# A state-space layer in a four-layer kernel: residual rows through TensorE, the norm's sums on ScalarE, two projections one slot sooner, one product moved from GpSimd to VectorE

## The chip, the cores and the metric

One core of a Trainium2 chip runs one program. The metric is the device time of a run in microseconds (us), the median over several runs. The core's engines are TensorE (PE in the profile; PEld is its weight load), VectorE (DVE), ScalarE (ACT), GpSimd (POOL) and SyncE (SP, which issues the DMAs). Engines work through their own instruction lists and meet only at semaphores.

## The reference, cut to what matters

The whole network is attention, a mixture of experts, a state-space layer and another mixture of experts on 8 sequences of 512 tokens by 256 features. The change is in the third, the state-space layer:

```python
h  = layernorm(layernorm(x)) * ln_g + ln_b           # over 256 features
xi, z = split(h @ W_in.T)                            # 512 channels each
u  = silu(conv4(xi) + conv_b)
dt, B, C = split(u @ W_x.T);  dt = softplus(dt @ W_dt + b_dt)
hst[t] = exp(dt[t] * A) * hst[t-1] + (dt[t] * u[t]) * B[t]     # 16 states for each channel
y[t] = sum over the 16 states of hst[t] * C[t]
out = x + (layernorm(x) + ((y + u * Dp) * silu(z)) @ W_out.T)
```

## The kernel before, in words

`mamba_phase` holds the layer. A **batch** m is one sequence (512 tokens; 8 batches). Its 512 channels are 4 channel tiles of 128 partitions, and the 16 states of a tile are 8 pairs, so a batch is 32 **units** of one tile and one pair of states; there are 256 units. The recurrence of a unit is one scan of VectorE over 2 x 512 elements.

A unit q passes these engines: ScalarE makes the decays `mb_da_ps` (L1817 to L1819: one zero, two Exp, two PSUM buffers taken in turn); GpSimd makes the added terms `mb_dbu` (L1769); VectorE scans; the scanned states are multiplied with C; TensorE sums the products into `mb_y_ps` (L1953: identity times product, two matmuls of 512 columns, each two records in the trace). The multiplication is done by VectorE (L1902 scan in place, L1908 product into `mb_hc`, two buffers) for pairs 0, 2, 4, 6 and 7, and by GpSimd (L1900 scan into `mb_hp`, three buffers, L1775 product) for pairs 1, 3 and 5.

Everything else of the layer is a list of small tasks, hung into the 32 **slots** of a batch by the table `SCHEDULE`: `(kind, index, ahead)`, where `ahead` says for which batch the task is (0: this one; 1: the next; 2: the one after it; -1: the last one). Every engine walks the same slots in order. TensorE does the tasks of a slot s after the sums of slot s (unit s-1 where VectorE multiplied, unit s-3 where GpSimd did); ScalarE does them after the decays of unit s+3, VectorE after unit s+3 (it is written `tasks(s - 3)` on VectorE, `tasks(s - 2)` on ScalarE). `EARLY_SCHEDULES` changes the table for the lead-in (n = -1) and the first batch (n = 0).

The kinds that matter here:

- `ln`: mean and variance of a batch's rows; `rsqrt`, `newton`, `norm_r`, `norm_h` follow. `norm_r` writes `mb_res`, the row that is to be added at the end; `norm_h` writes the normed input over `mb_xin`.
- `tr` 0 and 1: TensorE transposes `mb_xin` (L1965, 4 blocks each), ScalarE and VectorE split the result into `mb_hT_hi` and `mb_hT_lo`.
- `xi` 0 to 3, `z` 0 to 3: input projections (L1972, 6 matmuls each); `conv_a`, `conv`: half a convolution each (L1976); `xd`, `dt`: the small projections.
- `dt` i: TensorE, then five ScalarE instructions, then three of VectorE (the last is L1936).
- `out_a`, `out`: output projection of the last batch, 4 matmuls of 256 columns each (L1989); after each pair VectorE adds the result to `mb_res` (L1940), and SP stores when both are added.
- `final` i: VectorE multiplies a tile's sum `mb_y_ps` with silu(z) (L1914). It needs all 8 units of the tile summed by TensorE. Final i belongs to slot 6, 14, 22 or 30, so VectorE does final 0, 1, 2 after units 9, 17, 25 and final 3 after unit 1 of the next batch.

All task matmuls write into two PSUM buffers `mb_f_ps` taken in turn, in the order of the table: a fill may start when the fill two before it has been read out (`f_used`). So the order of the table decides which engine's reading a fill waits for.

Of the kernel before, what the change touches and what calls it, by code (L numbers as in the profile page):

```python
# [1635 lines left out]
LATER = (("z", 0, 1), ("z", 1, 1), ("z", 2, 1), ("z", 3, 1), ("norm_h", 0, 2), ("silu_z", 0, 1))
MOVED = {24: LATER[4:5], 25: LATER[0:2], 26: LATER[2:4]}
EARLY_SCHEDULES = {-1: {at: [task for task in SCHEDULE[at] if task not in LATER] + list(MOVED.get(at, ())) for at in SCHEDULE},
                   0: {at: SCHEDULE[at] + [("silu_z", 0, 0)] * (at == 1) for at in SCHEDULE}}
# [3 lines left out]
def mamba_phase(nc, sem, A, layer, x_in, x_out):  # L1643

    with ExitStack() as ctx:
# [78 lines left out]
        with nc.Block() as block:  # L1724
# [159 lines left out]
            def _(dve):  # L1884
# [5 lines left out]
                for s in SLOTS:  # L1890
# [18 lines left out]
                    for kind, i, m in tasks(s - 3):  # L1909
# [5 lines left out]
                        if kind == "ln":  # L1915
                            dve.wait_ge(S["x_loaded"], 16 * (m + 1))
                            wait(dve, S["h_ready"], m)
                            for k in range(4):
                                dve.bn_stats(stats[:, k, :], xin[:, k, :]).then_inc(S["stats_done"], 1)
                            dve.wait_ge(S["stats_done"], 4 * m + 4)  # L1920
                            for k in range(4):
                                last = dve.bn_aggr(mv[:, k, :], stats[:, k, :])
# [160 lines left out]
```

## Time and profile before

| | us |
|---|---|
| median of 3 runs | 2292.87 |
| lowest, highest | 2292.38, 2293.6 |
| the profiled execution: its own time | 2300.35 |
| the profiled execution: span of the trace | 2298.6 |

The profiled execution is 7.5 us (0.33%) above the median of the runs. Busy shares of its span: TensorE 84%, VectorE 74%, GpSimd 62%, ScalarE 52%. The state-space layer lies from 1015.6 to about 1998 us. Its loop over the units starts with the first scan at 1081.7 us and ends with the last final at 1988.8 us. Before it stands the lead-in (norms, projections and convolution of batch 0, transposes of batch 1), after it the last output projection.

Timeline rows give start, duration, engine, line, operation, tiles, shapes, how many instructions are merged, and in brackets the idle time of the engine before the row with what ended it. The distance between the starts of two rows on one engine is what the first one costs that engine's list.

### The profile page before, as it was taken

What the parts mean: (1) busy time and instruction counts of PE and PEld (TensorE: products, weight loads), DVE (VectorE), ACT (ScalarE), POOL (GpSimd) and SP (SyncE); (2) the same over time, 40 slices, a digit from 0 to 9 for tenths busy, and PEclk for the clock granted to TensorE, in tenths of its full rate; (3) what the DMA queues carried; (4) which work ended last, traced back from release to release, by engine and by line L of the source; (5) the groups of instructions that cost most, each with busy time, mean ns of one, the idle gap of its engine ahead of it and who ended that gap; (6) DMA issues with size and microseconds to landing.
All of it is one profiled execution on the core that took longest, in us unless ns stands there. A gap on an engine that the chain in (4) does not pass through costs nothing. (4 is left out here: it accounts for less than half of the span.)

```text
span 2298.6 us, 32626 instructions
## 1 busy us (share of the span) xinstructions
PE 1941.0 (84%) x9846; PEld 1136.6 (49%) x9846; DVE 1694.2 (74%) x2406; ACT 1198.6 (52%) x2466; POOL 1430.1 (62%) x1164
## 2 busy tenths in 40 slices
PE   2499999999873999947989898989898987569998
PEld 1234444444433999933444444444444433257776
DVE  4488777787744656522999999999999999655654
ACT  1066666666652433325676767676767574223222
POOL 7334435543342444422999999999999999444444
PEclk9699989898876999978999999999999999879999
DMA  3554444453143544424040404040404040101110
GB/s 81 103 110 101 103 96 108 111 124 100 51 153 127 100 70 75 76 39 157 0 148 19 148 19 148 19 148 19 148 19 148 10 148 9 60 7 37 36 36 19
DMA packets 231216, 185.57 MB, mean 81 GB/s; under 512 B 148729, under 2 KB 201601, under 8 KB 231058
## 3 DMA queue, kind: packets, MB, share of 16 engines
q1 hardware_dynamic: 216178, 162.61, 25.1%
q0 software_dynamic: 13296, 17.77, 4.4%
q10 hardware_dynamic: 1584, 3.24, 0.4%
q8 instruction: 80, 1.31, 0.2%
q14 instruction: 78, 0.64, 0.1%
HBM read 134.07 MB, written 49.49 MB: 80 GB/s over the span
## 5 line engine op out<-in xcount | busy, mean ns | idle before, releaser
L1769 POOL TENSOR_TENSOR mb_dbu<-mb_dtu,mb_bbc 128x1024 f32<-128x1024 f32 x256 | 600.4, 2361 | 41.8 <-DVE mb_hp L1900 29.6
L473 ACT ACTIVATE ex_plain<-at_t_ps 128x512 f32<-128x512 f32 x512 | 289.4, 595 | 185.9 <-PE at_t_ps L851 180.7
L1902 DVE TENSOR_TENSOR_SCAN mb_da_ps<-mb_da_ps,mb_dbu 128x1024 f32<-128x1024 f32 x160 | 365.3, 2283 | 12.6 <-ACT mb_da_ps L1819 12.6
L1953 PE MATMUL mb_y_ps<-mb_hc,lw_ident 128*128 128x512 f32 x640 | 323.9, 631 | 57.2 <-DVE mb_hc L1908 57.2
L610 DVE TENSOR_REDUCE at_mx<-at_s_ps 128x2 f32<-128x1024 f32 x256 | 310.8, 1219 | 51.4 <-PE at_s_ps L860 49.1
L860 PE MATMUL at_s_ps<-ex_w 48*128 48x512 f32 x512 | 228.1, 507 | 38.4 <-DVE at_mx L610 24.9
L851 PE MATMUL at_t_ps<-ex_w 64*128 64x512 f32 x512 | 221.7, 490 | 12.6 <-ACT ex_plain L473 6.7
L1953 PEld LDWEIGHTS mb_y_ps<-mb_hc,lw_ident 128*128 128x128 f32 x640 | 123.7, 199 | 215.7 <-issue 127.0
L1775 POOL TENSOR_TENSOR mb_hp<-mb_hp,mb_cbc 128x1024 f32<-128x1024 f32 x96 | 226.6, 2361 | 0.0
...
L1900 DVE TENSOR_TENSOR_SCAN mb_hp<-mb_da_ps,mb_dbu 128x1024 f32<-128x1024 f32 x96 | 218.8, 2279 | 2.5 <-ACT mb_da_ps L1819 2.5
L1908 DVE TENSOR_TENSOR mb_hc<-mb_da_ps,mb_cbc 128x1024 f32<-128x1024 f32 x160 | 196.0, 1225 | 18.3 <-DVE mb_da_ps L1902 0.5
L1817 ACT ACTIVATE mb_da_ps<-mb_zero 128x1 f32<-128x1 f32 x256 | 43.3, 169 | 289.0 <-DVE mb_hc L1908 240.2
L1953 PE MATMUL mb_y_ps<-mb_hp,lw_ident 128*128 128x512 f32 x384 | 190.9, 621 | 0.0
L851 PEld LDWEIGHTS at_t_ps<-ex_w 64*128 64x128 f32 x512 | 87.6, 195 | 172.7 <-ACT ex_plain L473 127.9
L1818 ACT ACTIVATE mb_da_ps<-mb_dt,lw_a_neg 128x512 f32<-128x512 f32 x256 | 172.5, 674 | 0.1
L1819 ACT ACTIVATE mb_da_ps<-mb_dt,lw_a_neg 128x511 f32<-128x511 f32 x256 | 171.8, 671 | 0.0
L1300 PE MATMUL m_y_ps<-ex_w,m_xsT_hi 128*128 x568 | 156.8, 337 | 0.0
L1415 POOL TENSOR_TENSOR m_odd<-m_odd,m_odd_in 128x256 f32<-128x256 f32 x96 | 70.8, 738 | 133.3 <-ACT m_odd_in L1473 130.0
L871 PE MATMUL at_o_ps<-ex_plain 128*32 128x512 f32 x1024 | 146.7, 646 | 0.1
L422 POOL CAST at_qk_hi<-at_qk 128x512 fp32r<-128x512 f32 x32 | 19.6, 611 | 185.8 <-DVE at_qk L754 185.8
L860 PEld LDWEIGHTS at_s_ps<-ex_w 48*128 48x128 f32 x512 | 89.6, 198 | 58.7 <-DVE at_mx L610 37.3
...
## 6 DMA issues: line engine op xcount, KB each, us to landing
...
```

The costliest lines, as they stand in the source:

```text
L473: act.activation(probs[:, c, h, :], t_ps[:, k % 2, :], ACT.Exp, scale=SCALE).then_inc(exp_done, 1)
L610: dve.tensor_reduce(out, s_ps[:, m % 2, :, :], AX.X, ALU.max).then_inc(max_done, 1)
L851: pe.matmul(t_ps[:, k % 2, :], of_head(kst, r, h, 64, c), of_head(qst, r, h, 64), start=True, stop=True).then_inc(t_ready, 1)
L860: last = pe.matmul(s_ps[:, m % 2, a, :], of_head(qst, u % 4, h + 2 * a, 48, c), of_head(kst, u % 4, h + 2 * a, 48), start=True, stop=True)
L1769: pool.tensor_tensor(dbu[:, q % 3, :, :], dtu_2, bbc[:, 2 * p:2 * p + 2, :], ALU.mult).then_inc(S["dbu_ready"], 1)
L1775: pool.tensor_tensor(hp[:, r, :, :], hp[:, r, :, :], cbc[:, 2 * p:2 * p + 2, :], ALU.mult).then_inc(S["hp_ready"], 1)
L1818: act.activation(da_ps[:, q % 2, 0, :], dt[:, d % 2, :], ACT.Exp, scale=a_neg[:, d, 2 * p:2 * p + 1])
L1819: act.activation(da_ps[:, q % 2, 1, 1:T], dt[:, d % 2, 1:T], ACT.Exp, scale=a_neg[:, d, 2 * p + 1:2 * p + 2]).then_inc(S["da_ready"], 1)
L1900: dve.tensor_tensor_scan(hp[:, t % 3, :, :].rearrange("p j t -> p (j t)"), da, add, 0.0, ALU.mult, ALU.add).then_inc(S["scan_done"], 1)
L1902: dve.tensor_tensor_scan(da, da, add, 0.0, ALU.mult, ALU.add).then_inc(S["scan_done"], 1)
L1908: dve.tensor_tensor(hc[:, t % 2, :, :], da_ps[:, r, :, :], cbc[:, 2 * p:2 * p + 2, :], ALU.mult).then_inc(S["hc_ready"], 1)
L1953: last = pe.matmul(y_ps[:, v % 2, :], ident[:, :], src[:, j, :], start=False, stop=(q == tile_last[v] and j == 1))
```

## The change

Four edits, all in `mamba_phase` and its table:

1. **The residual row.** TensorE starts each group of output matmuls with one more matmul, identity times the rows of `mb_res` (256 columns), so the PSUM result holds the sum already. VectorE's addition (L1940) goes; ScalarE copies the result into `mb_res` instead, in its own slot order.
2. **The norm's sums.** VectorE's `bn_stats` and `bn_aggr` (L1919, L1922) go. ScalarE takes sums as a by-product of three instructions for each of the four row blocks: a Copy with scale 1/256 whose sum is the mean, a small one for minus the mean over 16, and a Square whose sum is the variance. They hang in slots 10 to 13, one block each, where before one `ln` task hung in slot 11.
3. **The table.** `xi` 0 and 1 of the batch after next go from slots 31 and 0 to 30 and 31; the transposes `tr` from slot 27 to 26; `z` 3 from slot 26 to 24, so ahead of `dt` 0 of slot 25.
4. **Who multiplies.** Unit 19 of each batch (tile 2, pair 3) goes from GpSimd to VectorE, which leaves GpSimd 11 of 32.

```diff
-POOL_PAIRS = (1, 3, 5)
+POOL_UNITS = tuple(q for q in range(NU) if q % NP in (1, 3, 5) and q != 19)
...
-    25: [("dt", 0, 1), ("bb", 2, 1), ("cb", 0, 1)], 26: [("z", 3, 1), ("bb", 3, 1), ("cb", 1, 1)], 27: [("tr", 0, 2), ("tr", 1, 2), ("bb", 4, 1), ("cb", 2, 1)],
+    25: [("dt", 0, 1), ("bb", 2, 1), ("cb", 0, 1)], 26: [("tr", 0, 2), ("tr", 1, 2), ("bb", 3, 1), ("cb", 1, 1)], 27: [("bb", 4, 1), ("cb", 2, 1)],
...
-    31: [("xi", 0, 2), ("cb", 6, 1), ("cb", 7, 1)],
+    31: [("xi", 1, 2), ("cb", 6, 1), ("cb", 7, 1)],
...
+MOVED = {24: [("norm_h", 0, 2)], 25: [("z", 0, 1), ("z", 1, 1)], 26: [("z", 2, 1), ("z", 3, 1)], 27: [("tr", 0, 2), ("tr", 1, 2)], 31: [("xi", 0, 2)]}
+LATER = [task for at in MOVED for task in MOVED[at]] + [("xi", 1, 2), ("silu_z", 0, 1)]
+EARLY_SCHEDULES = {-1: {at: [task for task in SCHEDULE[at] if task not in LATER] + MOVED.get(at, []) for at in SCHEDULE},
+                   0: {at: [("xi", 1, 1)] * (at == 1) + SCHEDULE[at] + [("silu_z", 0, 0)] * (at == 1) for at in SCHEDULE}}
...
         def by_pool(q):
-            return q % NP in POOL_PAIRS
+            return q % NU in POOL_UNITS
...
@@ ScalarE
+                        if kind == "ln":
+                            act.wait_ge(S["x_loaded"], 16 * (m + 1))
+                            wait(act, S["x_stored"], 16 * (m - 2))
+                            act.activation(res[:, m % 3, i, :], xin[:, i, :], ACT.Copy, scale=1.0 / D, accum_out=mv[:, i, 0:1]).then_inc(S["stats_done"], 1)
+                            act.wait_ge(S["stats_done"], 12 * m + 3 * i + 1)
+                            act.activation(nm[:, i:i + 1], mv[:, i, 0:1], ACT.Copy, scale=-1.0 / 16.0).then_inc(S["stats_done"], 1)
+                            act.wait_ge(S["stats_done"], 12 * m + 3 * i + 2)
+                            act.activation(res[:, m % 3, i, :], xin[:, i, :], ACT.Square, scale=1.0 / 16.0, bias=nm[:, i:i + 1], accum_out=mv[:, i, 1:2]).then_inc(S["stats_done"], 1)
                         if kind == "rsqrt":
-                            act.wait_ge(S["var_ready"], m + 1)
+                            act.wait_ge(S["stats_done"], 12 * m + 12)
...
+                        if kind == "out":
+                            f, used = filled(act, "out", i, m)
+                            act.activation(res[:, m % 3, 2 * i:2 * i + 2, :], f.rearrange("p (a c) -> p a c", a=2), ACT.Copy).then_inc(used, 1)
@@ VectorE
-                        if kind == "ln":
...
-                        if kind == "out":
-                            f, used = filled(dve, "out", i, m)
-                            r_2 = res[:, m % 3, 2 * i:2 * i + 2, :]
-                            dve.tensor_tensor(r_2, f.rearrange("p (a c) -> p a c", a=2), r_2, ALU.add).then_inc(used, 1)
@@ TensorE
                         if whole == "out":
+                            pe.matmul(out[:, a * D:(a + 1) * D], ident[:, :], res[:, m % 3, 2 * i + a, :], start=True, stop=False)
                             for d in range(ND):
-                                last = pe.matmul(out[:, a * D:(a + 1) * D], u[:, m % 2, d, tok], wo[:, d, :], start=(d == 0), stop=(d == ND - 1))
+                                last = pe.matmul(out[:, a * D:(a + 1) * D], u[:, m % 2, d, tok], wo[:, d, :], start=False, stop=(d == ND - 1))
```

TensorE's list around the transposes, in a batch of the loop, before. `mb_hc` rows are sums of VectorE's products, `mb_hp` rows of GpSimd's, the row from `mb_xin` is the eight transposes:

```order
L1972 MATMUL mb_f_ps<-mb_hT_lo,lw_wi_hi 128x512
L1953 MATMUL mb_y_ps<-mb_hc,lw_ident 128x512 x2
L1965 MATMUL mb_f_ps<-lw_ident,mb_xin 128x128 x8
L1953 MATMUL mb_y_ps<-mb_hp,lw_ident 128x512 x2
L1953 MATMUL mb_y_ps<-mb_hc,lw_ident 128x512 x2
```

The same place after the change, with the last row ahead of the transposes being `dt` 0:

```order
L1948 MATMUL mb_y_ps<-mb_u,lw_diag_d 128x512
L1951 MATMUL mb_y_ps<-mb_hc,lw_ident 128x512 x2
L1981 MATMUL mb_f_ps<-mb_xd,lw_wdt 128x512
L1963 MATMUL mb_f_ps<-lw_ident,mb_xin 128x128 x8
L1951 MATMUL mb_y_ps<-mb_hc,lw_ident 128x512 x2
L1951 MATMUL mb_y_ps<-mb_hp,lw_ident 128x512 x2
```

The sum of unit 26 stood ahead of the transposes and now stands behind them; `z` 3 has gone ahead of `dt` 0.

TensorE's list at the turn to the next batch, before: the sums of units 31 and 29, which complete tile 3, then the six matmuls of `xi` 1, then the next tile's first matmul:

```order
L1953 MATMUL mb_y_ps<-mb_hc,lw_ident 128x512 x2
L1953 MATMUL mb_y_ps<-mb_hp,lw_ident 128x512 x2
L1972 MATMUL mb_f_ps<-mb_hT_hi,lw_wi_hi 128x512
L1972 MATMUL mb_f_ps<-mb_hT_hi,lw_wi_lo 128x512
L1972 MATMUL mb_f_ps<-mb_hT_lo,lw_wi_hi 128x512
L1972 MATMUL mb_f_ps<-mb_hT_hi,lw_wi_hi 128x512
L1972 MATMUL mb_f_ps<-mb_hT_hi,lw_wi_lo 128x512
L1972 MATMUL mb_f_ps<-mb_hT_lo,lw_wi_hi 128x512
L1950 MATMUL mb_y_ps<-mb_u,lw_diag_d 128x512
```

The same place after, from the sum of unit 30 on:

```order
L1951 MATMUL mb_y_ps<-mb_hc,lw_ident 128x512 x2
L1970 MATMUL mb_f_ps<-mb_hT_hi,lw_wi_hi 128x512
L1970 MATMUL mb_f_ps<-mb_hT_hi,lw_wi_lo 128x512
L1970 MATMUL mb_f_ps<-mb_hT_lo,lw_wi_hi 128x512
L1970 MATMUL mb_f_ps<-mb_hT_hi,lw_wi_hi 128x512
L1970 MATMUL mb_f_ps<-mb_hT_hi,lw_wi_lo 128x512
L1970 MATMUL mb_f_ps<-mb_hT_lo,lw_wi_hi 128x512
L1951 MATMUL mb_y_ps<-mb_hc,lw_ident 128x512 x2
L1951 MATMUL mb_y_ps<-mb_hp,lw_ident 128x512 x2
L1948 MATMUL mb_y_ps<-mb_u,lw_diag_d 128x512
```

`xi` 1 stood behind the sums of units 31 and 29 and now stands ahead of them.

TensorE's list at the end of the output projection of a batch, before:

```order
L1989 MATMUL mb_f_ps<-lw_wo,mb_u 128x256 x4
L1953 MATMUL mb_y_ps<-mb_hc,lw_ident 128x512 x2
L1989 MATMUL mb_f_ps<-lw_wo,mb_u 128x256 x4
L1953 MATMUL mb_y_ps<-mb_hp,lw_ident 128x512 x2
L1976 MATMUL mb_f_ps<-mb_xi,lw_diag 128x512 x2
```

and after:

```order
L1986 MATMUL mb_f_ps<-mb_res,lw_ident 128x256
L1988 MATMUL mb_f_ps<-lw_wo,mb_u 128x256 x4
L1951 MATMUL mb_y_ps<-mb_hc,lw_ident 128x512 x2
L1986 MATMUL mb_f_ps<-mb_res,lw_ident 128x256
L1988 MATMUL mb_f_ps<-lw_wo,mb_u 128x256 x4
L1951 MATMUL mb_y_ps<-mb_hp,lw_ident 128x512 x2
L1974 MATMUL mb_f_ps<-mb_xi,lw_diag 128x512 x2
```

One matmul of 256 columns has come in ahead of each group of four; nothing else has moved there.

## Rows read from the trace of the kernel before

**Rows 1.** Busy time by stretch: PE, PEld, DVE, ACT, POOL; clock, DMA share, GB/s

```profile
1230.00:1258.00 28.00, 28.00 (x73) 13.23 (x72) 27.38 (x25) 17.46 (x38) 27.28 (x15) 1.00 0.08 23
1298.00:1316.00 18.00, 16.39 (x43) 9.02 (x44) 17.59 (x14) 13.31 (x24) 16.20 (x9) 0.81 0.67 238
```

**Rows 2.** Waits from 1100 to 1990 us: total us, times, longest

```profile
ACT mb_da_ps L1817 <- DVE mb_hc L1908: 236.3, 112, 4.2
```

**Rows 3.** Timeline of VectorE, units 13 to 15 of a batch

```profile
1585.05 2.28 DVE L1900 TENSOR_TENSOR_SCAN mb_hp<-mb_da_ps,mb_dbu 128x1024 f32<-128x1024 f32 x1
1587.25 2.27 DVE L1902 TENSOR_TENSOR_SCAN mb_da_ps<-mb_da_ps,mb_dbu 128x1024 f32<-128x1024 f32 x1
1589.62 1.23 DVE L1908 TENSOR_TENSOR mb_hc<-mb_da_ps,mb_cbc 128x1024 f32<-128x1024 f32 x1
1590.76 1.40 DVE L1919 BATCH_NORM_STATS2 mb_stats<-mb_xin 128x6 f32<-128x256 f32 x4
...
1592.49 2.26 DVE L1902 TENSOR_TENSOR_SCAN mb_da_ps<-mb_da_ps,mb_dbu 128x1024 f32<-128x1024 f32 x1
```

**Rows 4.** Timeline from dt 1 to final 0 of the same batch

```profile
1556.32 0.69 DVE L1936 TENSOR_TENSOR mb_dt<-mb_f_ps,mb_dt 128x512 f32<-128x512 f32 x1
...
1557.06 1.99 PE L1989 MATMUL mb_f_ps<-lw_wo,mb_u 128*128 128x256 f32 x8 [0.81 <-DVE mb_dt L1936]
...
1562.67 0.68 DVE L1940 TENSOR_TENSOR mb_res<-mb_f_ps,mb_res 128x512 f32<-128x512 f32 x1
...
1570.92 1.88 PE L1953 MATMUL mb_y_ps<-mb_hp,lw_ident 128*128 128x512 f32 x4
...
1573.16 0.66 DVE L1914 TENSOR_TENSOR mb_u<-mb_y_ps,mb_z 128x512 f32<-128x512 f32 x1
```

**Rows 5.** Timeline at final 1: tile 1's last sum, and the final

```profile
1597.97 1.88 PE L1953 MATMUL mb_y_ps<-mb_hp,lw_ident 128*128 128x512 f32 x4
...
1601.73 0.67 DVE L1914 TENSOR_TENSOR mb_u<-mb_y_ps,mb_z 128x512 f32<-128x512 f32 x1
```

**Rows 6.** Timeline from dt 0 to final 3: transposes, tile 3's last sum

```profile
1641.66 0.69 DVE L1936 TENSOR_TENSOR mb_dt<-mb_f_ps,mb_dt 128x512 f32<-128x512 f32 x1
...
1642.40 1.97 PE L1965 MATMUL mb_f_ps<-lw_ident,mb_xin 128*128 128x128 f32 x8 [5.37 <-DVE mb_dt L1936]
...
1650.51 1.88 PE L1953 MATMUL mb_y_ps<-mb_hc,lw_ident 128*128 128x512 f32 x4
...
1653.61 1.88 PE L1953 MATMUL mb_y_ps<-mb_hc,lw_ident 128*128 128x512 f32 x4
...
1655.33 1.88 PE L1953 MATMUL mb_y_ps<-mb_hp,lw_ident 128*128 128x512 f32 x4
...
1658.47 0.67 DVE L1914 TENSOR_TENSOR mb_u<-mb_y_ps,mb_z 128x512 f32<-128x512 f32 x1
```

**Rows 7.** The same two anchors in an earlier batch

```profile
1298.87 0.69 DVE L1936 TENSOR_TENSOR mb_dt<-mb_f_ps,mb_dt 128x512 f32<-128x512 f32 x1
...
1313.27 1.88 PE L1953 MATMUL mb_y_ps<-mb_hp,lw_ident 128*128 128x512 f32 x4
```

**Rows 8.** Timeline at the end of the layer's loop

```profile
1986.87 1.88 PE L1953 MATMUL mb_y_ps<-mb_hp,lw_ident 128*128 128x512 f32 x4
1988.79 0.69 DVE L1914 TENSOR_TENSOR mb_u<-mb_y_ps,mb_z 128x512 f32<-128x512 f32 x1 [3.79 <-PE mb_y_ps L1953]
1989.63 7.14 PE L1989 MATMUL mb_f_ps<-lw_wo,mb_u 128*128 128x256 f32 x32 [0.87 <-DVE mb_u L1914]
```

**Rows 9.** Timeline of ScalarE: a norm_r task, four row blocks

```profile
1607.35 2.06 ACT L1833 ACTIVATE mb_res<-mb_xin,mb_nb,mb_up 128x256 f32<-128x256 f32 x4
```

**Rows 10.** Timeline of the lead-in: batch 0's sums, first reader, first late scan

```profile
1019.51 1.41 DVE L1919 BATCH_NORM_STATS2 mb_stats<-mb_xin 128x6 f32<-128x256 f32 x4 [2.07 <-DMA mb_xin<-x]
...
1021.45 0.30 ACT L1823 ACTIVATE mb_av<-mb_mv,mb_fix 128x4 f32<-128x4 f32 x1 [4.23 <-DVE mb_mv L1922]
...
1101.32 2.29 DVE L1900 TENSOR_TENSOR_SCAN mb_hp<-mb_da_ps,mb_dbu 128x1024 f32<-128x1024 f32 x1 [2.47 <-ACT mb_da_ps L1819]
```

More of the change, by code:

```diff
@@ L1622 @@
 NU = ND * NP
-POOL_PAIRS = (1, 3, 5)
+POOL_UNITS = tuple(q for q in range(NU) if q % NP in (1, 3, 5) and q != 19)
 SCHEDULE = {
-    0: [("xi", 1, 1)], 1: [("dt", 1, 0)], 2: [("out_a", 0, -1)], 3: [("out", 0, -1)], 4: [("out_a", 1, -1)], 5: [("out", 1, -1)],
-    6: [("conv_a", 0, 1), ("final", 0, 0)], 7: [("conv", 0, 1)], 8: [("dt", 2, 0), ("load", 0, 2)], 9: [("conv_a", 1, 1)], 10: [("conv", 1, 1)],
-    11: [("xi", 2, 1), ("ln", 0, 2)], 12: [("xi", 3, 1)], 13: [("z", 0, 1), ("newton", 0, 2)], 14: [("conv_a", 2, 1), ("final", 1, 0), ("rsqrt", 0, 2)],
+    1: [("dt", 1, 0)], 2: [("out_a", 0, -1)], 3: [("out", 0, -1)], 4: [("out_a", 1, -1)], 5: [("out", 1, -1)],
+    6: [("conv_a", 0, 1), ("final", 0, 0)], 7: [("conv", 0, 1)], 8: [("dt", 2, 0), ("load", 0, 2)], 9: [("conv_a", 1, 1)], 10: [("conv", 1, 1), ("ln", 0, 2)],
+    11: [("xi", 2, 1), ("ln", 1, 2)], 12: [("xi", 3, 1), ("ln", 2, 2)], 13: [("z", 0, 1), ("ln", 3, 2), ("newton", 0, 2)], 14: [("conv_a", 2, 1), ("final", 1, 0), ("rsqrt", 0, 2)],
     15: [("conv", 2, 1)], 16: [("dt", 3, 0)], 17: [("conv_a", 3, 1), ("norm_r", 0, 2)], 18: [("conv", 3, 1)], 19: [("silu_u", 0, 1)],
[4 rows of a table removed]
-}
[L1636 to L1639, printed above, removed]
[4 rows of a table added]
+}
+MOVED = {24: [("norm_h", 0, 2)], 25: [("z", 0, 1), ("z", 1, 1)], 26: [("z", 2, 1), ("z", 3, 1)], 27: [("tr", 0, 2), ("tr", 1, 2)], 31: [("xi", 0, 2)]}
+LATER = [task for at in MOVED for task in MOVED[at]] + [("xi", 1, 2), ("silu_z", 0, 1)]
+EARLY_SCHEDULES = {-1: {at: [task for task in SCHEDULE[at] if task not in LATER] + MOVED.get(at, []) for at in SCHEDULE},
+                   0: {at: [("xi", 1, 1)] * (at == 1) + SCHEDULE[at] + [("silu_z", 0, 0)] * (at == 1) for at in SCHEDULE}}
 FILL_KINDS = ("out", "z", "dt", "tr", "xi", "conv", "xd")
@@ L1652, in mamba_phase @@
         res = sb("res", [P, 3, 4, D])
-        stats, mv = sb("stats", [P, 4, 6]), sb("mv", [P, 4, 2])
+        mv, nm = sb("mv", [P, 4, 2]), sb("nm", [P, 4])
         av, lv, rs, tv, nb = (sb(q, [P, 2, 4]) for q in ("av", "lv", "rs", "tv", "nb"))
@@ L1701, in by_pool @@
         def by_pool(q):
-            return q % NP in POOL_PAIRS
+            return q % NU in POOL_UNITS
         def turn(q):
-            return sum(by_pool(v) == by_pool(q) for v in range(q % NP)) + (q // NP) * (len(POOL_PAIRS) if by_pool(q) else NP - len(POOL_PAIRS))
+            return sum(by_pool(v) == by_pool(q) for v in range(q % NU)) + (q // NU) * (len(POOL_UNITS) if by_pool(q) else NU - len(POOL_UNITS))
         def multiplied(eng, q):
@@ L1914, in _ @@
                             dve.tensor_tensor(u[:, m % 2, i, :], y_ps[:, v % 2, :], z[:, v % 5, :], ALU.mult).then_inc(S["yg_ready"], 1)
-                        if kind == "ln":
[L1916 to L1922, printed above, removed]
-                            last.then_inc(S["var_ready"], 1)
                         if kind == "tr":
```

2 lines of the change are left out of this document (1 added, 1 removed), and 4 rows, old and new, of the table SCHEDULE.

## The prediction, as put on record before the changed kernel was run

> **What bounds the kernel now.** I read the page's shares first, then busy time by stretch inside the state-space layer, then the waits, then the timeline between the points where TensorE and VectorE meet. The page puts TensorE and VectorE ahead of the others; the stretches say more: from 1230 to 1258 us TensorE is busy for all 28.00 us at full clock and VectorE for 27.38 [rows 1]. Both run nearly without a gap, so taking work from one is worth something only where the other has room. VectorE makes the pace: a unit that GpSimd multiplies costs it 2.20 us (1585.05 to 1587.25), one that it multiplies itself 3.51 (1587.25 to 1590.76) [rows 3]. ScalarE waits 112 times for VectorE's product, 236 us in all [rows 2]; it has room. TensorE meets VectorE at the four finals of a batch. A sum's result reaches VectorE 1.92 us after the sum starts: where VectorE had to wait for it, 1986.87 against 1988.79 [rows 8]. By that:
>
> - final 0: ready 1570.92 + 1.92 = 1572.84, VectorE comes at 1573.16: 0.32 us of room [rows 4];
> - final 1: ready 1597.97 + 1.92 = 1599.89, VectorE at 1601.73: 1.84 us of room [rows 5];
> - final 3: ready 1655.33 + 1.92 = 1657.25, VectorE at 1658.47: 1.22 us [rows 6]. VectorE comes 16.81 us after its last dt row; TensorE's last sum starts 13.67 us after it here and 14.40 in another batch [rows 6, 7], so the room there is 1.2 and 0.5 us; about 1.0 is taken for the six batches that have transposes.
>
> Both engines start each of these stretches together: `out_a` 1 waits for the buffer of dt 1 (0.81 us, at 1557.06) [rows 4], the transposes for that of dt 0 (5.37 us, at 1642.40) [rows 6]. TensorE can't get ahead before these points, so what it has to do behind them counts in full.
>
> **The change part by part,** against the profiled execution's 2300.35 us, which is 7.5 us above the median of 2292.87; the differences are carried to the median.
>
> *Unit 19 to VectorE.* Of a unit that VectorE multiplies, 3.51 - 2.20 = 1.31 us are the product's [rows 3]: in 8 batches +10.5 us. It lies between final 1 and final 2, where TensorE has 1.84 us of room and nothing hides it. GpSimd gets a product back, and no one waits for it there: worth nothing.
>
> *The norm's sums off VectorE.* 1590.76 to 1592.49 is 1.73 us [rows 3], in the six batches that prepare another: 10.4 us. TensorE limits this. From the last sum ahead of final 0 to that ahead of final 1 it needs 1570.92 to 1597.97 = 27.05 us, and VectorE from final to final 28.57, without the sums 26.84 [rows 4, 5]. Once final 0 waits for TensorE (next edit), both start together, and 0.2 us comes back at final 1: 6 x 1.52 = -9.1 us.
>
> *The residual row.* VectorE saves two additions between dt 1 and final 0; a row of 0.68 us [rows 4], of which some 0.08 overlaps what follows (as 1.23 against 1.14 at 1589.62 [rows 3]): 0.60 us each. TensorE gets four matmuls of 256 columns a batch. Its 16 matmuls at the layer's end take 7.14 us for 32 records [rows 8], so one costs about 0.43 us. Two of the four stand behind the point at 1557.06. Counted from the dt row at 1556.32, the sum is then ready after 1572.84 + 0.86 - 1556.32 = 17.38 us; VectorE comes after 16.84 - 1.20 = 15.64 [rows 4]. TensorE now ends last, and final 0 is 0.54 us later than before instead of 1.20 sooner. That holds for n = 1 to 6; in the last batch no convolution of a next one stands there, and 1.20 is saved. 6 x 0.54 - 1.20 = +2.0 us. ScalarE's two copies lie in its idle time and free the buffers sooner than VectorE did; uncovered they would be 0.7 us each.
>
> *The table.* `tr` 0 now uses the buffer of `z` 3 and can be done early, but `tr` 1 uses that of `dt` 0 and waits for the same VectorE instruction as before. In front of it stood the sum of unit 26; now that stands behind. `xi` 1 stood behind the sums that complete tile 3; now it stands ahead of them. A sum is 1.72 us (1653.61 to 1655.33), a sum and a projection 3.10 (1650.51 to 1653.61), so the projection 1.38 [rows 6]. Between the dt row and final 3 TensorE gains 3.10 us and loses four transposes, at most half of 1.97 [rows 6]: net 2.1 to 3.1, taken at 2.5, against 1.0 us of room. VectorE waits 1.5 us (1.1 to 2.1) at final 3, in six batches: +9.0 us. Behind that wait stands all of VectorE's list, and with it ScalarE's next decays. ScalarE's copy of `tr` 1 now stands ahead of the decays of unit 30; VectorE does its two `tr` instructions one unit sooner, which gives ScalarE that time.
>
> TensorE's clock enters here. In the 18 us around these sums the granted clock is 0.81 of 2.4 GHz on the mean [rows 1], behind the idle stretch ahead of the transposes; some records run at 1.2 GHz. After the change the idle stretch is about 1 us longer, so I keep that loss as it is.
>
> *The norm's sums on ScalarE.* In the trace no instruction of ScalarE gives a sum. Nearest row: 256 columns, 2.06 us for four, so about 0.5 us apart [rows 9]. A block is two of these and a small one, with two waits on its own results: at least 1.1 us, at most 1.7 if the sum has to be fetched; I take 1.3, nearer the low end, since that row is the same pass over the data. In the loop a block of up to 2.1 us fits between a decay that is released and the next that is due (two units of 3.5 us, less two sets of decays and an evacuation), and costs nothing. In the lead-in it is on the path: batch 0's sums took 1019.51 to 1021.45 = 1.94 us [rows 10] and become 5.2 us (4.4 to 6.8): +3.3. Batch 1's stand ahead of two evacuations and of norm_r, partly in idle time: half their 5.2 us, +2.4 (1 to 5). `xi` 1 of batch 1 moves into the slot in which ScalarE is late by 2.47 us already (scan at 1101.32) [rows 10]: +0.6. Together +6.3 us (3 to 12).
>
> The Trainium skill, "ScalarE: Activation LUTs", section "What ACT_TABLE_LOAD costs", gives an ACTIVATE 186 ns and 0.833 ns a column, and 93 ns for each operand that is a column. By it a block would be 1.08 us and the whole sum about 1.5 us lower. For the row of norm_r it makes 585 ns, which agrees with 2.06 us for four that overlap; of sums it says no price, and no row here has one.
>
> *The end of the layer.* Four more matmuls of 0.43 us behind the last final: +1.7 us.
>
> Sum: 10.5 - 9.1 + 2.0 + 9.0 + 6.3 + 1.7 = +20.4 us; 2292.87 + 20.4 = 2313.3, put at 2313.
>
> **Rivals.**
>
> 1. *TensorE has the room after all* (not slower). The place is final 0 and final 3: if the added matmuls and the moved sum and projection fit ahead of VectorE there, its list decides, which in the loop gets shorter by 10.4 (sums) + 7 x 1.20 (additions) - 10.5 = 8.3 us. With +6.3 and +1.7 outside the loop: 2292.6. It decides once the room at final 0 is 0.86 + 1.20 = 2.1 us and that at final 3 is 2.5. For it: TensorE's rows overlap (a row of 1.88 us, 1.72 to the next), so a busy share is too high a measure. Against it: the starts, which don't overlap, leave 0.32 us [rows 4]. The Trainium skill, "Trainium Kernel Development and Optimization", section "Performance Expectations", calls matmul busy time a bad metric for the distance to the roofline and takes LDWEIGHTS busy time instead. That is 13.23 of 28 us here [rows 1], and by that rule this rival holds.
> 2. *ScalarE becomes late* (slower still). If a block costs over 2.1 us, four slots in a row run behind and the scans wait: at 2.5 us about 0.4 x 3 x 6 = 7 us in the loop and 8 more in the lead-in: 2328. For it: the sums' cost isn't in the trace. Against it: 236 us of ScalarE's waits [rows 2].
> 3. *The table's moves cost nothing*, because TensorE catches up before final 3 (its clock not falling): 20.4 - 9.0: 2304. Against it: the idle stretch ahead of the transposes is still there.
>
> **How the numbers follow.** Forecast 0.66, rival 1 0.18, rival 2 0.10, rival 3 0.06. The forecast's own bounds: lead-in -3 to +6, table -2 to +4, finals 0 and 1 -4 to +2: some 2303 to 2322. With rival 3 and half of rival 2 the range is 2297 to 2328. A difference under 0.2% (4.6 us) can't be told from none. Slower by more: 0.81; within: 0.12, most of it rival 1; faster by more: 0.07, rival 1 with a cheap lead-in.
>
> **What would show it.** VectorE waits for `mb_y_ps` at final 0 (about 1.7 us, n = 1 to 6), at final 1 (0.2) and at final 3 (about 1.5), some 18 times in the loop; a batch gets 1.31 - 1.52 + 0.54 + 1.5 = 1.8 us longer; the second four transposes start right behind a dt row with TensorE idle for 6 us ahead of them; the rows with sums stay near 0.5 us; the first scan is 6 us later. It is wrong if VectorE's finals start without a wait (rival 1), if its scans wait for the decays in the slots of the sums (rival 2), or if the rows with sums cost over 0.7 us each.

## The result and the profile after

The kernel after takes 2306.95 us (median; 2304.91 to 2308.89 over 4 runs), the kernel before beside it 2292.62: ratio 1.0069, 95% interval 1.0057 to 1.0081. It is slower, by 14.3 us; forecast were 20.4 us and 2313, with a range from 2297 to 2328. The time lies 6 us under the forecast and 3 us above the 2304 of rival 3, so it does not choose between them; the waits have to. The profiled execution has 2307.15 us, its span 2305.4.

Three points cut the state-space layer in both traces: ScalarE's first table load (the layer starts), the first scan, the last final; the store of the last rows ends it. All stretches run from the start of one such row to the start of the next.

| us | before | after | difference | predicted |
|---|---|---|---|---|
| lead-in | 66.05 | 70.21 | +4.2 | +5.7 |
| loop (first scan to last final) | 907.08 | 918.47 | +11.4 | +13.0 |
| end (last final to store) | 8.74 | 10.37 | +1.6 | +1.7 |
| layer | 981.87 | 999.05 | +17.2 | +20.4 |

The late `xi` 1 (+0.6), which the prediction counts with the lead-in, lies behind the first scan, so it stands with the loop here: 12.4 + 0.6 = 13.0, and 5.7 are left for the lead-in.

The layers around it run the same instructions; in the profiled executions what lies ahead differs by 10.6 us the other way, and over the fourteen traces of this case the layer starts anywhere from 1004.2 to 1015.7 us. The end stretch repeats within 0.01 us, the lead-in within 1.2 among kernels that have the same tasks there. The loop was traced once for each kernel, and the part of it that hangs on TensorE's clock moves: the waits at and just ahead of final 3 sum to 8.4, 8.8, 9.9, 10.5 and 11.1 us in five kernels with the new table. So the stretches tell more than the ratios, but a difference of under 3 us in the loop can be the clock's.

In the kernel after, VectorE waits for TensorE at the finals. The waits from 1100 to 1990 us, totals, times, longest:

```profile
DVE mb_u L1925 <- PE mb_y_ps L1951: 17.6, 12, 1.7
DVE mb_da_ps L1913 <- ACT mb_da_ps L1819: 12.1, 8, 1.7
DVE mb_hc L1919 <- PE mb_y_ps L1951: 3.4, 5, 0.9
```

The middle row is old: it is the silu of the next batch's `u`. The other two are finals, and products whose buffer TensorE still reads.

From dt 1 to final 0, the timeline that answers to [rows 4]:

```profile
1555.04 0.69 DVE L1938 TENSOR_TENSOR mb_dt<-mb_f_ps,mb_dt 128x512 f32<-128x512 f32 x1
...
1555.78 0.70 PE L1986 MATMUL mb_f_ps<-mb_res,lw_ident 128*128 128x256 f32 x2 [0.58 <-DVE mb_dt L1938]
1556.32 1.89 PE L1988 MATMUL mb_f_ps<-lw_wo,mb_u 128*128 128x256 f32 x8
...
1559.76 0.60 PE L1986 MATMUL mb_f_ps<-mb_res,lw_ident 128*128 128x256 f32 x2
1560.19 1.89 PE L1988 MATMUL mb_f_ps<-lw_wo,mb_u 128*128 128x256 f32 x8
...
1570.51 1.88 PE L1951 MATMUL mb_y_ps<-mb_hp,lw_ident 128*128 128x512 f32 x4
1572.42 0.69 DVE L1925 TENSOR_TENSOR mb_u<-mb_y_ps,mb_z 128x512 f32<-128x512 f32 x1 [1.66 <-PE mb_y_ps L1951]
```

From the dt row to final 0 are 17.38 us, as worked out, and the wait is 1.66 in all six batches (forecast 1.7). A residual matmul costs the list 0.43 us (1559.76 to 1560.19).

At final 1 the two engines arrive together. The sum starts at 1597.40, ready by the 1.92 us of [rows 8] at 1599.32, and there VectorE starts, without a wait:

```profile
1597.40 1.88 PE L1951 MATMUL mb_y_ps<-mb_hp,lw_ident 128*128 128x512 f32 x4
1599.32 0.69 DVE L1925 TENSOR_TENSOR mb_u<-mb_y_ps,mb_z 128x512 f32<-128x512 f32 x1
```

From dt 0 to final 3, answering to [rows 6]:

```profile
1640.62 0.69 DVE L1938 TENSOR_TENSOR mb_dt<-mb_f_ps,mb_dt 128x512 f32<-128x512 f32 x1
...
1641.36 1.11 PE L1963 MATMUL mb_f_ps<-lw_ident,mb_xin 128*128 128x128 f32 x4 [6.67 <-DVE mb_dt L1938]
1642.27 3.62 PE L1951 MATMUL mb_y_ps<-mb_hc,lw_ident 128*128 128x512 f32 x4
1645.68 2.54 PE L1951 MATMUL mb_y_ps<-mb_hp,lw_ident 128*128 128x512 f32 x4
1648.06 1.88 PE L1951 MATMUL mb_y_ps<-mb_hc,lw_ident 128*128 128x512 f32 x4
...
1654.88 1.23 DVE L1919 TENSOR_TENSOR mb_hc<-mb_da_ps,mb_cbc 128x1024 f32<-128x1024 f32 x1 [0.92 <-PE mb_y_ps L1951]
...
1657.73 1.88 PE L1951 MATMUL mb_y_ps<-mb_hp,lw_ident 128*128 128x512 f32 x4
1659.65 0.69 DVE L1925 TENSOR_TENSOR mb_u<-mb_y_ps,mb_z 128x512 f32<-128x512 f32 x1 [1.35 <-PE mb_y_ps L1951]
```

The last sum starts 17.11 us after the dt row, before 13.67: 3.44 more. With 1.22 us of room 2.22 are left, and VectorE waits 0.92 + 1.35 = 2.27. The sum of unit 26, moved behind TensorE's idle stretch, takes 3.41 us (1642.27 to 1645.68) instead of 1.72. The granted clock (the column after POOL's) is 0.50 there, which is 1.2 GHz:

```profile
1642.27:1645.68 3.41, 3.41 (x5) 1.35 (x5) 3.41 (x4) 3.17 (x7) 3.33 (x3) 0.50 0.99 322
```

This is one of the dearer batches. Over the six, the last sum starts 13.87 us after the dt row before (13.10 to 14.54) and 16.78 after (15.97 to 17.13): 2.9 more, against 1.0 of room, and VectorE waits 1.9. Part of the 2.9 is the clock. From the dt row to the last sum it was at 1.2 GHz for 5.22 us a batch before and for 5.73 after (worked out from the mean granted clock of each stretch), and a sum took twice as long there, 3.41 us against 1.72. Without half of that time 11.26 and 13.92 us are left. The traces of a, e and f below, with the old table, give 11.23 to 11.30 in the same way, those of b, c, d and i, with the new one, 13.90 to 13.92. So the new order costs 2.66 us a batch, and the clock 0.26 on top in this trace.

A block of sums on ScalarE, in the lead-in:

```profile
1010.17 0.40 ACT L1824 ACTIVATE mb_res<-mb_xin 128x256 f32<-128x256 f32 x1
1010.48 0.19 ACT L1824 ACTIVATION_READ_ACCUMULATOR mb_res<-mb_xin 128x1 f32 x1
1010.69 0.20 ACT L1826 ACTIVATE mb_nm<-mb_mv 128x1 f32<-128x1 f32 x1
1010.93 0.51 ACT L1828 ACTIVATE mb_res<-mb_xin,mb_nm 128x256 f32<-128x256 f32 x1
1011.34 0.19 ACT L1828 ACTIVATION_READ_ACCUMULATOR mb_res<-mb_xin,mb_nm 128x1 f32 x1
1011.44 0.40 ACT L1824 ACTIVATE mb_res<-mb_xin 128x256 f32<-128x256 f32 x1
```

It costs 1.27 us (1010.17 to 1011.44; 1.3 forecast). Batch 0's sums take 1008.89 to 1014.10 = 5.21 us.

### The profile page after: what moved, and what is told of

The parts are those of the page before. It is cut to its first block and busy times, and to the rows that moved or that the text cites. A ratio compares the mean times of both kernels' runs of the same rounds, so it can differ in the third digit from the quotient of the medians.

```text
span 2305.4 us, 32870 instructions
## 1 busy us (share of the span) xinstructions
PE 1944.8 (84%) x9910; PEld 1142.1 (50%) x9910; DVE 1681.3 (73%) x2334; ACT 1243.8 (54%) x2642; POOL 1411.7 (61%) x1156
## 5 line engine op out<-in xcount | busy, mean ns | idle before, releaser
L1913 DVE TENSOR_TENSOR_SCAN mb_da_ps<-mb_da_ps,mb_dbu 128x1024 f32<-128x1024 f32 x168 | 383.8, 2284 | 12.7 <-ACT mb_da_ps L1819 12.6
L1951 PE MATMUL mb_y_ps<-mb_hc,lw_ident 128*128 128x512 f32 x672 | 342.4, 637 | 42.6 <-DVE mb_hc L1919 42.6
L1951 PEld LDWEIGHTS mb_y_ps<-mb_hc,lw_ident 128*128 128x128 f32 x672 | 131.1, 201 | 207.3 <-issue 134.7
L851 PE MATMUL at_t_ps<-ex_w 64*128 64x512 f32 x512 | 220.1, 487 | 11.6 <-ACT ex_plain L473 6.4
L1919 DVE TENSOR_TENSOR mb_hc<-mb_da_ps,mb_cbc 128x1024 f32<-128x1024 f32 x168 | 205.8, 1225 | 21.4 <-PE mb_y_ps L1951 3.4
L1775 POOL TENSOR_TENSOR mb_hp<-mb_hp,mb_cbc 128x1024 f32<-128x1024 f32 x88 | 207.5, 2358 | 0.0
L1911 DVE TENSOR_TENSOR_SCAN mb_hp<-mb_da_ps,mb_dbu 128x1024 f32<-128x1024 f32 x88 | 200.6, 2280 | 3.0 <-ACT mb_da_ps L1819 3.0
L1951 PE MATMUL mb_y_ps<-mb_hp,lw_ident 128*128 128x512 f32 x352 | 169.4, 604 | 0.0
L1974 PE MATMUL mb_f_ps<-mb_xi,lw_diag 128*128 128x512 f32 x256 | 117.2, 592 | 0.0
```

The lines of the kernel that those rows point to most:

```text
L851: pe.matmul(t_ps[:, k % 2, :], of_head(kst, r, h, 64, c), of_head(qst, r, h, 64), start=True, stop=True).then_inc(t_ready, 1)
L1775: pool.tensor_tensor(hp[:, r, :, :], hp[:, r, :, :], cbc[:, 2 * p:2 * p + 2, :], ALU.mult).then_inc(S["hp_ready"], 1)
L1911: dve.tensor_tensor_scan(hp[:, t % 3, :, :].rearrange("p j t -> p (j t)"), da, add, 0.0, ALU.mult, ALU.add).then_inc(S["scan_done"], 1)
L1913: dve.tensor_tensor_scan(da, da, add, 0.0, ALU.mult, ALU.add).then_inc(S["scan_done"], 1)
L1919: dve.tensor_tensor(hc[:, t % 2, :, :], da_ps[:, r, :, :], cbc[:, 2 * p:2 * p + 2, :], ALU.mult).then_inc(S["hc_ready"], 1)
L1951: last = pe.matmul(y_ps[:, v % 2, :], ident[:, :], src[:, j, :], start=False, stop=(q == tile_last[v] and j == 1))
```

## The experiments

Theory: the slowdown is four separate terms (unit 19, the table, the lead-in, and little from the residual row), less what the sums give. Rivals are with each run. Letters a to d undo one edit each, g and h half of the table edit, i and l move the product, e and f go to a better version, j and k try to go past it. Each was timed in 5 rounds beside the kernel before; the stretches, in us, are those of one traced execution of each:

| kernel | lead-in | loop | end | layer less before's | ratio, 95% interval |
|---|---|---|---|---|---|
| before | 66.05 | 907.08 | 8.74 | | |
| after | 70.21 | 918.47 | 10.37 | +17.2 | 1.0069 (1.0057 to 1.0081) |
| a, old table | 69.54 | 906.85 | 10.37 | +4.9 | 1.0018 (1.0006 to 1.0031) |
| b, VectorE adds | 70.71 | 915.64 | 8.74 | +13.2 | 1.0056 (1.0041 to 1.0072) |
| c, unit 19 back | 70.10 | 906.49 | 10.36 | +5.1 | 1.0024 (1.0012 to 1.0035) |
| d, sums on VectorE | 65.88 | 928.52 | 10.37 | +22.9 | 1.0116 (1.0096 to 1.0136) |
| e, a and c | 69.97 | 896.34 | 10.37 | -5.2 | 0.9978 (0.9963 to 0.9993) |
| f, before and late sums | 66.14 | 893.14 | 8.74 | -13.9 | 0.9944 (0.9925 to 0.9963) |
| g, only xi back | 69.99 | 910.91 | 10.37 | +9.4 | 1.0045 (1.0028 to 1.0062) |
| h, only tr back | 69.60 | 909.90 | 10.37 | +8.0 | 1.0033 (1.0019 to 1.0047) |
| i, unit 21 for 19 | 70.26 | 906.92 | 10.37 | +5.7 | 1.0020 (1.0011 to 1.0029) |
| j, silu later, xd 23 | 66.60 | 899.56 | 8.74 | -7.0 | 0.9969 (0.9958 to 0.9980) |
| k, silu later, xd 22 | 66.88 | 898.32 | 8.74 | -7.9 | 0.9953 (0.9938 to 0.9968) |
| l, unit 19 alone | 66.81 | 914.90 | 8.74 | +8.6 | 1.0043 (1.0028 to 1.0058) |

**a.**

```diff
-    24: [("scr", 0, 1), ("z", 3, 1), ...], 26: [("tr", 0, 2), ("tr", 1, 2), ...], 30: [("xi", 0, 2), ("final", 3, 0), ...], 31: [("xi", 1, 2), ...],
+    0: [("xi", 1, 1)], 24: [("scr", 0, 1), ...], 26: [("z", 3, 1), ...], 27: [("tr", 0, 2), ("tr", 1, 2), ...], 30: [("final", 3, 0), ...], 31: [("xi", 0, 2), ...],
```

> The kernel after with the table of the kernel before (xi 0 and 1 in slots 31 and 0, z 3 in 26, tr in 27); the four blocks of sums stay in slots 10 to 13. Theory (TensorE's list ends last at final 3 because the sum of unit 26 and xi 1 stand ahead of tile 3's last sums): the waits at and just ahead of final 3, 11.1 us in the trace of the kernel after, go, and xi 1 leaves the late first slot of the lead-in (-0.6): 2306.95 - 11.7 = 2295, with final 0 still waiting 1.7 us. Rival (VectorE meets TensorE somewhere else then, because its list is shorter by the norm's sums): the wait comes back at final 0 or 1, the time stays within 3 us of 2307.

The loop is 11.6 us shorter, the waits at and ahead of final 3 (11.1 us) are gone, final 0 still waits 1.66 to 1.73, and only 0.5 us at two products came in their place. The scan behind the late `xi` 1 waits 2.47 us again instead of 3.04; it lies behind the first scan, so the 0.7 us by which the lead-in is shorter is not that, but lies within the lead-in's scatter. The rival falls: this edit cost what the waits at final 3 showed.

**b.**

```diff
-                            pe.matmul(out[:, a * D:(a + 1) * D], ident[:, :], res[:, m % 3, 2 * i + a, :], start=True, stop=False)
+                            dve.tensor_tensor(r_2, f.rearrange("p (a c) -> p a c", a=2), r_2, ALU.add).then_inc(used, 1)
```

> The kernel after with the residual row added by VectorE again, and TensorE without the four matmuls of identity times mb_res. Theory (the matmuls sit on TensorE's path to final 0): the wait of 1.66 us at final 0 goes and VectorE does 1.20 us more there: final 0 comes 0.5 us sooner in six batches (-3.2), the last batch pays 1.2, the layer's end saves 1.6: -3.6 us, 2303.4. Rival (matmuls of 256 columns overlap and cost nothing there, VectorE's list decides): 7 x 1.2 = +8.4, -1.6 at the end: 2313.8.

2.8 us less in the loop and 1.6 at the end are 4.4, against 3.6 by the theory; the lead-in, which has no output projection, is 0.5 longer by scatter. The mechanism is the theory's: final 0 has no wait any more. The rival falls. From final 3 to the next final 0 are 28.21 us in b and 28.75 in the kernel after, in six batches, and 28.18 and 26.99 in the last: 6 x 0.54 - 1.19 = 2.05 of the 2.8. The rest stands at final 3, where the waits hang on the clock.

**c.**

```diff
-POOL_UNITS = tuple(q for q in range(NU) if q % NP in (1, 3, 5) and q != 19)
+POOL_UNITS = tuple(q for q in range(NU) if q % NP in (1, 3, 5))
```

> The kernel after with unit 19 multiplied by GpSimd again. Theory (a product costs VectorE's list 1.31 us and nobody waits for GpSimd): 8 x 1.31 = -10.5 us at most; final 2 has no wait in the trace of the kernel after, before it had two of 0.4 and 1.4 us, so some 2 us may stay as a wait there: 2296.5 to 2298.5. Rival (VectorE's 1.31 us is taken up by a wait for TensorE at final 2 in every batch): within 3 us of 2307. Rival (GpSimd, with a product more, is late for sums or scans): no gain or slower.

12.0 us less: the 10.5 of the product and, against expectation, no wait at final 2, but 2.7 us less of waits at and just ahead of final 3, and 1.0 more at final 0 of batch 0. The 2.7 go with the clock, which is at 1.2 GHz for 4.96 us a batch ahead of final 3 where it was for 5.73; TensorE's idle stretch is the same 6.67 us in both, so that the edit caused this is not shown. Both rivals fall.

**d.** The norm's sums as `bn_stats` and `bn_aggr` on VectorE, slot 11.

> The kernel after with the norm's sums as bn_stats and bn_aggr on VectorE in slot 11. Theory: 6 x 1.73 = +10.4 us in the loop (no wait at final 1 in the trace of the kernel after, so all of it counts), -4.2 in the lead-in: 2313. By the prediction's own terms (9.1 back, 5.7 saved): 2310.4. Rival (the loop doesn't gain from it, since TensorE sets the pace from final 0 to final 1): 2303.

Loop +10.05, lead-in -4.3: the sums off VectorE do pay in the loop, and TensorE does not set the pace there. The ratio says more than the stretches (+10.8 us against +5.7 from the kernel after); its interval is 9 us wide. Ahead of the sum of unit 20 TensorE now idles 1.9 us, with 0.6 to 0.9 more just before. Over the next 7 us the granted clock is 0.76 in three of the six batches and 1.00 in the others, and final 2 waits in none: with unit 19 on VectorE there is room for it.

**g and h.** The table's two halves.

```diff
g: +    0: [("xi", 1, 1)], ..., 31: [("xi", 0, 2), ...]       (z 3 in 24, tr in 26 as after)
h: +    27: [("tr", 0, 2), ("tr", 1, 2), ...]                 (z 3 in 24, xi in 30 and 31 as after)
```

> The kernel after with xi 0 and 1 back in slots 31 and 0; z 3 stays in 24 and tr in 26. Theory (xi 1 is 1.38 us of TensorE's list ahead of tile 3's last sums): 6 x 1.38 = 8.3 us less waiting at final 3, and 0.6 in the lead-in: 2298; what is left at final 3 is 0.5 us a batch. Rival (the sum behind the transposes is the whole cost): 2306.

> The kernel after with tr back in slot 27, so the sum of unit 26 ahead of the transposes again; z 3 stays in 24, xi 0 and 1 in 30 and 31. Theory (the sum fits into TensorE's idle time ahead of the transposes, 1.72 us, against half of the transposes, 1.0 us, that are no longer done early): 0.7 to 1.7 us a batch less at final 3, 4 to 10 us, 2297 to 2303. With the run that has only xi back the two gains are to add up to the 11.7 us of the whole table. Rival (xi 1 is the whole cost): 2307.

Loop -7.6 and -8.6, both together (a) -11.6. Each is as large as expected; that they add up was wrong: a wait of 1.9 us a batch can't be taken away twice. Either half alone nearly fits into TensorE's room at final 3. Without the clock, as worked out above, the last sum comes 1.39 us sooner than in the kernel after in g and 1.48 in h. So `xi` 1 costs its 1.38, but the four transposes done early give back only some 0.2 us of the sum's 1.72, not 1.0.

**i and l.** Which product, and the product alone.

```diff
i: +POOL_UNITS = tuple(q for q in range(NU) if q % NP in (1, 3, 5) and q != 21)
l: before, with POOL_UNITS without 19
```

> The kernel after with unit 21 instead of unit 19 multiplied by VectorE; GpSimd has 11 units as there. Behind unit 22 VectorE waits 1.67 us in every batch for the decays that ScalarE makes after silu_u. Theory (the product of unit 21 stands ahead of that wait, the silu behind the product of unit 20, which stays where it is): the product's 1.31 us goes into the wait, which falls to 0.36, and the edit costs nothing: 10.5 us less than the kernel after, the loop near 908, the ratio to the kernel before near 1.002. Rival (any product on VectorE costs its 1.31 us, or the silu moves with it): as the kernel after, ratio 1.007.

> The kernel before with only unit 19 moved to VectorE. Theory: 8 x 1.31 = +10.5 us, less the 2.7 us that final 2 waited for TensorE in four batches: +8 to +10.5, ratio 1.0035 to 1.0046. Rival (TensorE's idle time at unit 20, 3.2 us before, gets 1.3 longer, its clock falls more often and final 2 waits more): above 1.005.

In i VectorE's wait behind unit 22 falls from 1.67 to 0.32 us, in each of seven batches:

```profile
1386.06 2.30 DVE L1913 TENSOR_TENSOR_SCAN mb_da_ps<-mb_da_ps,mb_dbu 128x1024 f32<-128x1024 f32 x1 [0.32 <-ACT mb_da_ps L1819]
```

and the loop is as with 12 units on GpSimd (906.92 against 906.49): a product ahead of a wait for another engine is free, two units earlier it costs 8 to 12 us. In l the loop is 7.8 longer: 10.5, less the 3.5 us of waits in the kernel before, which are gone (2.65 at final 2 and 0.8 at two products), and 0.9 of new waits at two products. The trace puts one of the old product waits (0.46) and both new ones down to VectorE's own scan, so that TensorE ended them is not shown. The rival falls as to the time: the clock over the 7 us behind the sum of unit 20 does fall, to 0.76 in three batches of six, but final 2 has no wait, and the ratio is 1.0043.

**e and f.** Two edits undone at once; and the kernel before with the sums of batches 2 to 7 alone:

```diff
f: +                        if kind == "ln" and m > 1:     (ScalarE, blocks in slots 10 to 13)
f: +                        if kind == "ln" and i == 0 and m < 2:     (VectorE, as before)
```

> The kernel after with both the table of the kernel before and unit 19 multiplied by GpSimd; the residual row and the norm's sums stay as in the kernel after. Theory (the two costs stand at different places, final 3 and units 17 to 25, and add up): the loop, 906.85 us with the old table alone, gets 8 x 1.31 = 10.5 shorter, 896.3; with a lead-in of 69.5 and an end of 10.4 the layer is 5.7 us shorter than in the kernel before: 2284.6 beside 2290.3. Rival (TensorE now sets the pace from final 1 to final 2 as well): a wait of up to 1.3 us at final 2 takes the gain back, 2290 to 2295.

> The kernel before with one thing changed: the norm's sums of batches 2 to 7 by ScalarE in slots 10 to 13; those of batches 0 and 1 stay bn_stats and bn_aggr on VectorE, so the lead-in is that of the kernel before. Theory: 1.73 us less on VectorE's list in six batches, 10.4 us, where TensorE has 1.84 us of room at final 1; in the four batches in which final 2 waited for TensorE already (0.4 to 1.4 us) some 1.5 us of it comes back there as a longer wait: 4 to 10 us less, 2280 to 2286. Rival (TensorE limits every batch, the sums only filled its shadow): 2290. Rival (the blocks of sums make ScalarE late): the scans wait for the decays, slower than 2290.

e: 896.34 as worked out; it beats the kernel before. f is the best version of all, 0.9944, and its loop is 13.9 us shorter where 4 to 10 were expected. From 1090 us to the last batch VectorE waits for ScalarE only, a batch takes 111.79 us (before 113.5 to 115.3), and final 2, where I expected longer waits, has none. The traces say why. TensorE idles ahead of the sum of unit 20, in the kernel before for 3.23 us:

```profile
1156.97 1.55 PE L1953 MATMUL mb_y_ps<-mb_hc,lw_ident 128*128 128x512 f32 x3 [3.23 <-DVE mb_hc L1908]
...
1384.47 2.07 PE L1953 MATMUL mb_y_ps<-mb_hc,lw_ident 128*128 128x512 f32 x2 [3.23 <-DVE mb_hc L1908]
```

In the 7 us from each of these, and from the row of f at the same place, busy times and granted clock. A mean of 0.57 or 0.76 is a stretch that was partly at 1.0 (2.4 GHz) and partly at 0.5 (1.2 GHz):

```profile
1156.97:1163.97 7.00, 7.00 (x19) 3.22 (x20) 5.56 (x3) 6.94 (x9) 7.00 (x5) 1.00 0.01 2
1384.47:1391.47 7.00, 7.00 (x13) 3.89 (x14) 5.55 (x3) 6.94 (x9) 7.00 (x5) 0.57 0.00 0
```

```profile
1369.30:1376.30 7.00, 7.00 (x19) 3.22 (x20) 5.56 (x3) 6.94 (x9) 7.00 (x4) 1.00 0.00 0
```

The finals 2 that follow in the kernel before:

```profile
1173.58 0.67 DVE L1914 TENSOR_TENSOR mb_u<-mb_y_ps,mb_z 128x512 f32<-128x512 f32 x1
...
1402.81 0.69 DVE L1914 TENSOR_TENSOR mb_u<-mb_y_ps,mb_z 128x512 f32<-128x512 f32 x1 [1.41 <-PE mb_y_ps L1953]
```

The same idle time in six batches, and the clock falls in some and not in others: in the two where it stayed at 1.00 final 2 did not wait, in the three with 0.76 it waited 0.41, 0.44 and 0.39, in the one with 0.57 1.41. The sums on VectorE, 1.73 us, are what made the idle time 3.23 instead of 1.52 us; in f it is 1.52 in the first seven batches and the clock over the next 7 us is 1.00 in all seven. So taking them away gives back the sums and the waits: 6 x 1.70 (final 0 to final 1 is 26.87 us, before 28.57) and the 3.5 us of waits, 13.7 of the 13.9 us. The 10.2 are read between the same two finals in six batches. The 3.5 come from one traced execution of the kernel before, and another can fall otherwise: by its ratio f is 12.8 us faster (8.5 to 17.2), which agrees with 10.4 as with 13.9. The kernel before has its own control: batch 6 prepares no further batch and has no sums; TensorE idles 1.52 us there and final 2 doesn't wait. The Trainium skill, "TensorE: Matmul & The Clock Gate", section "Part 1: The HAM clock gate", says that the array's clock follows how busy it was recently; the trace agrees in that the slow rows shown stand behind idle time. Equal idle times ended in different clocks here.

**j and k.** From f on, to take VectorE's 1.67 us behind silu_u as well.

```diff
-    19: [("silu_u", 0, 1)], 20: [("norm_h", 0, 2)], 22: [("xd", 0, 1), ...], 23: [("z", 2, 1)]
+j:  20: [("silu_u", 0, 1)], 21: [("z", 1, 1), ("norm_h", 0, 2)], 22: [("z", 2, 1), ...], 23: [("xd", 0, 1)]
+k:  20 and 21 as in j, xd in 22, z 2 in 23
```

> The kernel of the run with the sums from batch 2 on, and in its table silu_u one slot later (20), norm_h in 21, z 2 in 22 and xd in 23. Theory (of VectorE's wait of 1.67 us behind unit 22, 1.31 goes: the decays of unit 23 are made ahead of the silu, and unit 23, which VectorE multiplies itself, gives 3.5 us instead of 2.2 until the next are due): 8 x 1.3 = 10.4 us less than that kernel, the loop near 883, ratio to the kernel before 0.990. Rival (xd and dt 0 come so late that scans or final 2 and 3 wait for them): 0.994 or above.

> The same with silu_u in slot 20 and norm_h in 21, but xd left in slot 22 and z 2 in 23. Theory: TensorE stands idle some 2 us more ahead of xd, with the sums of units 22 and 23 behind it, so final 2 waits 1 to 2 us and part of the gain goes: ratio 0.991 to 0.995. Rival (TensorE catches up before final 2): 0.990, as with xd in 23.

A miss: 0.9969 for j, where 0.990 was expected, and 0.9953 for k. The wait behind unit 22 does fall to 0.3 us, but TensorE stands 1.84 us ahead of `xd` in k, and final 2 waits:

```profile
1379.90 3.60 PE L1992 MATMUL mb_f_ps<-mb_u,lw_wx 128*49 128x512 f32 x8 [1.84 <-ACT mb_u L1862]
```

```profile
1390.30 0.69 DVE L1926 TENSOR_TENSOR mb_u<-mb_y_ps,mb_z 128x512 f32<-128x512 f32 x1 [1.42 <-PE mb_y_ps L1965]
```

With 0.67 more at a product, 2.1 us a batch come for the 1.3 that went; in j 1.79 at final 2 and 0.23 at a scan. The loop of j is 6.4 us longer than f's, that of k 5.2; the ratios of f and k are too close to tell them apart. VectorE's wait had been TensorE's time to catch up.

## Why the prediction was right, and where its terms were off

Going from the kernel before to the one after by way of f, e and c, one edit at a time, the loop changes by -13.9 (sums), +3.2 (residual row), +10.2 (table; the old one still in e), +12.0 (unit 19; still on GpSimd in c): +11.4. The edits share waits and clock, so in another order the sizes differ. By the prediction's steps:

- *Unit 19 to VectorE*, +10.5: right in mechanism. 7.8 alone, 12.0 last, 10.5 of it the product; the rest is in waits of finals 2 and 3 that come or go beside it. That "no one waits for it there" held: VectorE never waits for GpSimd, and TensorE's weight loads do for 2.1 us in all before and 1.6 after. Overlooked was that final 2 waited in four batches of the kernel before (2.65 us), where the prediction reads room, and that another unit would have been free.
- *The norm's sums off VectorE*, -9.1: right way, too small. -13.9 put in first (of which 3.5 as one trace had them), 10.05 back when undone last. The 0.2 us held back for final 1 was not needed: TensorE goes from the last sum ahead of final 0 to that ahead of final 1 in 26.89 us, not 27.05, and the engines meet there exactly. The step "TensorE limits this" left out that a shorter list of VectorE shortens TensorE's idle time, and with it what the clock takes.
- *The residual row*, +2.0: right; 2.05 between final 3 and final 0 by b (2.8 in the whole loop, 3.2 from f to e), with the wait of 1.66 us at final 0 in each of the six batches.
- *The table*, +9.0, and +0.6 for the late `xi` 1: right place, too small; 11.6 by a, 10.2 from e to c, both with `xi` 1. Waits at final 3 and the product ahead of it are 0.89 to 2.27 us a batch, 11.1 in sum. The room was as read, 1.0 us. Off were the net 2.5 us, which is 2.66, because the early transposes save TensorE 0.44 us and not the 0.6 that was taken off, and "I keep that loss as it is": the clock took 0.26 us a batch more. That the longer idle stretch did this (6.67 us, before 5.2 to 5.4) is not shown: c and i, with 6.67 and 7.19, had the clock at 1.2 GHz for 4.96 and 5.04 us a batch, less than the 5.22 of the kernel before.
- *The norm's sums on ScalarE*, +6.3: block right (1.27 against 1.3), batch 0's +3.3 measured as 5.21 - 1.94 = 3.27, `xi` 1 in the late slot +0.57 (3.04 against 2.47). At the silu's table load the lead-in is 5.5 us late, near the forecast, at the first scan only 4.2. From that table load to the first scan:

```profile
1054.33:1081.71 27.38, 17.04 (x44) 9.01 (x45) 3.47 (x6) 14.97 (x24) 8.30 (x4) 0.75 0.54 193
1049.26:1075.31 26.05, 15.70 (x44) 8.40 (x45) 3.48 (x6) 14.97 (x24) 8.32 (x4) 0.80 0.54 191
```

  The kernel before takes 27.38 us at a mean clock of 0.75, the one after 26.05 at 0.80, and `xd` at the start of the stretch 6.19 and 5.53 us. This is no luck: in the six traces with these sums on VectorE the stretch takes 27.35 to 27.81 us and TensorE idles 4.4 us ahead of `xd`, in the eight with them on ScalarE 25.78 to 26.20 and 6.2 us; d, which undoes only the sums, is back at 27.35. So the edit also gives back 1.3 us in the lead-in, by TensorE's clock, a term that the prediction doesn't have. Why the clock is back sooner behind the longer idle time stays open.
- *The end*, +1.7: 1.63, with the same wait of 3.79 us at the last final as in [rows 8].

In the loop the errors of two terms partly cancel, the sums (-9.1 for at least -10.05) and the table (+9.6 for 10.2 to 11.6); that the loop came out at 11.4 against 13.0 owes something to luck. So 3.2 us of the 6.1 between 20.4 and 14.3 are the terms above; the remaining 2.9 lie outside the layer or in the scatter of the runs, and stay open. The bounds given add up to 2304 and 2325, not 2303 and 2322. Rival 1 (TensorE has the room) falls with every wait shown; TensorE's weight loads are busy 13.36 of 28 us at a place where its list is exactly as long as VectorE's:

```profile
1225.00:1253.00 28.00, 28.00 (x73) 13.36 (x72) 27.09 (x19) 21.80 (x58) 26.58 (x17) 1.00 0.00 0
```

The row answers to [rows 1]. The Trainium skill, "Trainium Kernel Development and Optimization", section "Performance Expectations", names MFU and LDWEIGHTS busy time as the measures of the distance to the roofline. Read as room in TensorE's list, as in rival 1, the 13.36 us would have left half of it free; the trace disagrees. Rival 2 (ScalarE late) falls: no scan of the loop waits for a decay in the slots of the sums. Rival 3 (table free) falls with a.
